# Counting drawn keys in a one-core decoder: VectorE adds pairs of one-hot rows before TensorE sums them

## What is computed

```
itok_BxSx64 = jax.random.randint(key, (8, 256, 64), 0, 512, jnp.int32)
c_kv = x_kv @ W_kv_down.T
c_sel = c_kv[jnp.arange(b)[:, None, None], indices]
kv = (c_sel @ W_kv_up.T).reshape(b, nq, K, 2, H, HD)
scores = jnp.einsum('bqhd,bqkhd->bqkh', q, k) * SCALE
attn = jax.nn.softmax(scores, axis=2)
out = jnp.einsum('bqkh,bqkhd->bqhd', attn, v)
```

## Time and profile before

| | |
|---|---|
| median of 3 runs | 2487.09 us (2479.24 to 2487.94) |
| profiled execution | 2495.8 us, its span 2493.9 us |
| TensorE matmuls busy | 2184.8 us, 88% of the span |
| VectorE busy | 1311.4 us, 53% |
| ScalarE busy | 1001.0 us, 40% |
| mean granted TensorE clock | 0.908 of full |
| one-hot rows, L2887 | 1024 instructions |
| count matmuls, L2905 | 1024 instructions |

### The profile page before, as it was taken

One profiled execution on the slowest core, in us unless ns is written; L12 is line 12 of the kernel. 1 busy time (PEld: TensorE's weight loads), 2 busy tenths in 40 slices (PEclk: granted clock), 3 DMA queues, 4 the chain that ended last, 5 costly groups with the idle time before them and its releaser, 6 DMA issues. The chain is left out here.

```text
span 2493.9 us, 39095 instructions
## 1 busy us (share of the span) xinstructions
PE 2184.8 (88%) x13679; PEld 1536.5 (62%) x13679; DVE 1311.4 (53%) x3911; ACT 1001.0 (40%) x3150; POOL 365.3 (15%) x639
## 2 busy tenths in 40 slices
PE   8588998998999988996557898999999999999986
PEld 4266666666777755776334565666666666666654
DVE  7236576575444455321137656656565665657441
ACT  3123555545443544442122344544444443444221
POOL 2044253352314051001000000000000000000000
PEclk9758999998998988998769899999999999999988
DMA  8000000002232012447540000000000000000000
GB/s 314 9 1 5 6 10 5 10 14 83 91 104 91 20 46 94 133 164 256 134 162 0 2 11 11 1 9 6 9 6 5 11 5 5 6 5 5 5 1 9
DMA packets 51051, 116.27 MB, mean 47 GB/s; under 512 B 8224, under 2 KB 30496, under 8 KB 47008
## 3 DMA queue, kind: packets, MB, share of 16 engines
q1 hardware_dynamic: 48880, 101.60, 12.3%
q10 hardware_dynamic: 432, 7.89, 0.8%
q0 software_dynamic: 1536, 4.20, 0.6%
HBM read 90.20 MB, written 23.46 MB: 46 GB/s over the span
## 5 line engine op out<-in xcount | busy, mean ns | idle before, releaser
L702 ACT ACTIVATE PRS<-PT 128x384 f32<-128x384 f32 (+1 forms) x512 | 265.9, 519 | 627.1 <-PE PT L633 626.9
L767 DVE TENSOR_REDUCE negmax<-SM 128x2 f32<-128x512 f32 x432 | 283.8, 686 | 213.9 <-PE SM L596 203.1
L633 PE MATMUL PT<-const_sb,PRS 128*128 128x128 f32 x1664 | 301.1, 297 | 55.9 <-ACT PRS L702 51.7
L717 ACT ACTIVATE PRS<-SM,negmax 128x128 f32<-128x128 f32 x608 | 248.1, 420 | 150.1 <-DVE negmax L767 147.1
L633 PEld LDWEIGHTS PT<-const_sb,PRS 128*128 128x128 f32 x1664 | 199.7, 149 | 150.5 <-issue 99.0
L2887 DVE TENSOR_SCALAR arena<-arena 128x256 bf16<-128x256 bf16 x1024 | 210.5, 280 | 9.0 <-PE SC L2905 8.0
L586 PE MATMUL SM<-haloU,QM 32*128 32x128 f32 (+1 forms) x1056 | 158.7, 359 | 4.4 <-ACT PRS L717 2.6
L2905 PE MATMUL SC<-arena,identb 128*128 128x256 bf16 x1024 | 138.4, 278 | 2.2 <-DVE arena L2887 2.2
L586 PEld LDWEIGHTS SM<-haloU,QM 32*128 32x128 f32 x1056 | 121.9, 205 | 17.7 <-issue 8.6
L648 PE MATMUL OA<-PRS,big 128*32 128x256 f32 (+1 forms) x1024 | 132.0, 382 | 0.9 <-ACT PRS L702 0.7
L717 ACT ACTIVATION_READ_ACCUMULATOR PRS<-SM,negmax 128x1 f32 x608 | 124.0, 204 | 0.0
(11 more groups left out here) (586 smaller groups left out, 4073.0 us busy)
## 6 DMA issues: line engine op xcount, KB each, us to landing
arena<-lay SPq DMA_DIRECT2D x50, 1024.0 KB, 4.9
rows<-OT SPq DMA_DIRECT2D x2, 3456.0 KB, 32.0
arena<-lay ACTq DMA_DIRECT2D x1, 5265.5 KB, 24.3
arena<-lay SPq DMA_DIRECT2D x1, 3862.0 KB, 19.6
arena<-rows SPq DMA_DIRECT2D x25, 128.0 KB, 2.6
arena<-lay SPq DMA_DIRECT2D x25, 128.0 KB, 5.2
rows<-arena SPq DMA_DIRECT2D x25, 128.0 KB, 4.4
rows<-OT SPq DMA_DIRECT2D x1, 2432.0 KB, 21.5
```

Of the source, the lines that this page charges most:

```text
L633: ins = pe.transpose(bank[:, o:o + P], PR[n % 4][:, t, k * P:(k + 1) * P], ident)
L702: act.activation(dst, src, ACT.Copy).then_inc(S("probs_moved"), 1)
L717: ins = act.activation(dst, src, ACT.Exp, bias=negmax[:, h, r:r + 1], accum_out=rsum[:, t, h:h + 1])
L767: st.post(dve.tensor_reduce(negmax[:, ORDER[s], :], two(banks[s % NB]), AX.X, ALU.max, negate=True), S("max_ready"))
```

## The change

VectorE still writes 8 one-hot rows. It then waits for itself (`settle`) and adds rows 4 to 7 onto rows 0 to 3, four pairs in one `tensor_tensor` of 128 x 1024 bf16 elements. TensorE sums the 4 rows that are left. The values are 0, 1 or 2, which bf16 holds exactly, so the counts are the same.

```diff
@@ -2885,7 +2885,10 @@
                 t, j0 = g // 8, g % 8 * 8
                 for j in range(8):
                     ins = dve.tensor_scalar(oneh[g % 2][:, j, :], iotab, idx[:, t, j0 + j:j0 + j + 1], None, ALU.is_equal)
-                    st.post(ins, S("hot_ready") if j == 7 else None)
+                    st.post(ins)
+                st.settle()
+                st.post(dve.tensor_tensor(oneh[g % 2][:, 0:4, :], oneh[g % 2][:, 0:4, :], oneh[g % 2][:, 4:8, :], ALU.add),
+                        S("hot_ready"))
                 yield
             yield
             dve.wait_ge(S("hot_used"), GROUPS_HOT * (i + 1))
@@ -2901,9 +2904,9 @@
             for g in range(GROUPS_HOT):
                 t, j0 = g // 8, g % 8 * 8
                 pe.wait_ge(S("hot_ready"), GROUPS_HOT * i + g + 1)
-                for j in range(8):
+                for j in range(4):
                     ins = pe.matmul(SC[:, t * T:(t + 1) * T], identb[:], oneh[g % 2][:, j, :],
-                                    start=j0 + j == 0, stop=j0 + j == NI - 1)
+                                    start=j0 + j == 0, stop=j0 + j == NI - 5)
                 ins.then_inc(S("hot_used"), 1)
                 yield
             yield
```

## The result

| | before | change |
|---|---|---|
| median, us | 2483.16 (4 runs, 2475.92 to 2487.94) | 2514.65 (4 runs, 2505.00 to 2521.95) |
| profiled execution, its span | 2495.8, 2493.9 | 2521.95, 2520.1 |
| mean granted clock | 0.908 | 0.894 |

The ratio is 1.0116, 95% interval 1.0067 to 1.0164: slower, by clearly less than 2%. The prediction was 2480 us, within 2463 to 2499.

What follows compares the result with a forecast made beforehand. TensorE was taken as the bound, with VectorE close behind in `tally(0)`. From the 2487.1 us median, +3.7 - 2.0 - 9.9 = -8.2 gave 2478.9, plus 1 for the clock: 2480 us, range 2463 to 2499.

Steps and rivals of the forecast that it cites:

- D: Time of the added VectorE addition per group: taken as 0.69 us, with 1.22 as the other bound.
- rival 2: The addition runs at the f32 rate, 1.22 us, so the kernel is slower: +24, 2511 us; 10 in 100.
- A slot of `tally(0)`: In batch 0's pass VectorE becomes the bound, and a slot grows from 5.09 to 5.82 us.
- The new wait at the end of later `tally` passes: TensorE reaches its count matmuls before the late group is ready and waits 1.95 us.
- The scores behind the norm: In later `tally` passes TensorE already idles 0.97 us there; the group on the path adds 0.74.
- -8.2 us: Whole-kernel sum before the clock allowance: +3.7 for `tally(0)`, -2.0 for batch 1, -9.9 for batches 2 to 7.
- the walk: Slot-by-slot carrying of TensorE's shift: batch 1 gains 2.0 us, batches 2 to 7 gain 1.65 each.
- The first pass: `tally(0)`: five slots +3.6 us, three groups behind them +2.2, two old waits give back 1.0 and 1.1; +3.7.
- 7 passes about -16: Count groups in later batches mostly keep their saving; in batch 4 `count(3)` moves the shift from +0.78 to -1.65 us.
- I add 1 us for the clock: Allowance for TensorE's granted clock over the whole kernel, raising 2478.9 us to the forecast 2480.
- rival 4: New waits near 1826 and 1860 lower TensorE's clock: four stretches at 1.7 us, +7, 2486 us; 10 in 100.
- clock theory: Set up after the result: the prediction's steps were right, and TensorE's lower clock level took the gain.

Runs made afterwards that it cites:

- second profile: The same changed kernel profiled and timed again beside the kernel before: 2498.8 us, ratio 1.0043.
- filler in waits: The changed kernel plus zero-weight matmuls only where TensorE waits for VectorE: 2491.0 us, ratio 1.0007 to the kernel before.
- count groups: The change for groups 9 to 15 of batches 1 to 7 only, against the kernel before, run twice: 2461.9 and 2469.2 us, ratios 0.9905 and 0.9940.
- set 2: Second set of follow-up timings, with the unaltered change run again: kernel before 2483.8 us, change 2498.8 us, ratio 1.0043.
- one row: TensorE sums 1 of the 8 rows and no addition is made, against the kernel before: 2438.5 us, ratio 0.9844.
- first pass: The change for batch 0 only, against the kernel before: 2494.8 us, ratio 1.0058.
- later `tally`: The change for groups 0 to 8 of batches 1 to 7 only, against the kernel before: 2499.3 us, ratio 1.0072.

## Why the prediction was wrong

**Right.** D: 0.694 us measured, 0.69 taken; rival 2, the f32 rate, is out. The Trainium skill (VectorE: DVE Perf Modes, The perf-mode tier table) gives bf16 `tensor_tensor` twice the f32 rate. The trace agrees: less the 0.15 us that don't grow with the size in the earlier trace rows (0.685 - 512 x 1.05 ns), the addition takes 0.53 ns an element against 1.05. My own argument for 0.69, by bytes and by the pitch of the one-hot rows, was a guess between two bounds that came out. A slot of `tally(0)`: 5.93 us measured from one pair of row maxima to the next (1413.65 less 1407.72), 5.82 worked out, and VectorE without idle time; the 0.1 is the wait on itself, which I took at 0.05 a group and which is 0.10 in the rows above (1405.36 + 1.65 to 1407.11). The new wait at the end of later `tally` passes: 2.07, and 1.95 worked out. The scores behind the norm: 1.73 of wait, and 0.97 + 0.74 = 1.71 worked out. As a whole: -8.2 us at an unchanged clock means 56.3 of work gone and 48.1 of waits come in; the stretch shows 44.5 (45 in the second profile).

Batches 1 to 7 by themselves: work -49.3 (448 matmuls) and waits +36.1, so -13.2 without the clock term, and -13.1 in the second profile; the walk had -2.0 - 9.9 = -11.9.

**Partly.** The first pass is 6.4 us longer where the clock is as before (filler in waits, 70.12 to 63.66), +3.7 predicted: the five slots cost 0.84 each, not 0.73; behind them 1.7 are added, not 1.1; and the two opening slots give nothing back where I had counted 1.0. With the later batches that makes 6.4 - 13.2 = -6.8 at an unchanged clock, near -8.2. The count groups keep 14 us at the full clock; the walk gave 7 passes about -16. The full-clock time of the whole change is -15, more than the sum's -8.2, but this product flatters a kernel with long waits.

**The step that failed** is the one sentence "I add 1 us for the clock", and with it the price of rival 4. I had named the mechanism and its place (waits near 1826 and 1860), gave it four stretches and +7 us, and a chance of 10 in 100. The clock term measured +24 and +31 us in the stretch. Of each, 5.6 us lie in the first pass, where they cost 0.5 us of time, so in time it is +18 and +26. Over all executions, the clock's share of the span is 217 us before and 245 in the change in set 2, 215 and 260 in the first runs: +28 and +45. That 45 also holds what the clock did in unchanged code, 0.85 behind the stretch against 0.88 before, which the change need not have caused., from which I took the price, were also misread: TensorE is busy for all 3.40 us of the stretch ahead of the fall, so they show no fall after light work. I had counted the waits, 48 us of them, for their own length alone, and for the clock had guessed a number of stretches in place of going through each new wait. The count of places was in my own working: about five slots in `tally(0)`, two or three in each of seven later passes, some twenty, where I took four. At my own price of 1.7 us a stretch, the measured 18 to 26 us are 11 to 15 stretches.

**What the parts say of the cause.** The clock term goes with TensorE's new waits, whatever made them. Kernels with 6 to 9 us of new waits have a term of -4 to +8, those with 18 to 27 us -2 to +14, those with 38 to 51 us +21 to +64; among the last are one with no addition (one row) and one with the addition on GpSimd. Matmuls placed in the waits bring the clock back. Four matmuls fewer alone (+9) and the addition alone (+9) lower it little. The parts by group: first pass +8, later `tally` +14, count groups 0 and -4, which is most of +24 and +31. So the time went to the clock, and the waits are what brought it down; the clock theory stands in this form, not in the form that fewer matmuls are enough. What stays open is which wait brings the clock down and which doesn't: in the changed kernel the stretch at 1850.0, with TensorE busy for 1.70 of 3.40 us, was not followed by a fall.

## What to carry to other kernels

When a change turns TensorE's work into TensorE's waits, even one for one, it can be a loss: price each new wait a second time for the clock, by going through the places. Halve the work only where the engine that pays has slack at that very place; here 49 to 77 of the 128 groups gave 11 to 22 us and the others took more than that back. To compare variants, look at span times mean clock beside the span: it scatters far less than the span, and tells schedule from clock as long as TensorE is the bound. Where another engine is, it shows too low a time, as in the first pass here.

## What the runs showed of the hardware

Span times mean granted clock is nearly constant for one kernel: 2266 to 2267 us on average for the kernel before in each of three sets of runs, single executions within some 7 us of it, with spans that differ by 23 to 36 us. The clock makes most of the scatter.

While GpSimd adds, VectorE's one-hot rows are slower: 313 ns on average, and 280 with GpSimd idle; the run of eight below takes 2.54 us, not 1.65. Of these the first row takes 1.17 us and ends at 1408.01, 0.08 us after the addition. Timeline of the GpSimd kernel:

```profile
1405.81 2.12 POOL L2901 TENSOR_TENSOR arena<-arena 128x1024 bf16<-128x1024 bf16 x1 [2.51 <-DVE arena L2887]
1406.84 2.54 DVE L2887 TENSOR_SCALAR arena<-arena 128x256 bf16<-128x256 bf16 x8 [1.11 <-PE SC L2915]
```

The Trainium skill (SBUF — State Buffer, SBUF: two separate sides) says that the two engines lock one shared pair of ports against each other; the rows agree that VectorE is held up, here with instructions of one tensor input.
